# A graph layer kernel: constants projected first, x3 and x5 on another queue, and another split of the last tile

## The reference, cut to what matters

```python
h = maximum(layernorm(x), 0.0)                        # rows
xn = batchnorm(h, norm1_g, norm1_b)                   # columns
agg = segment_sum(xn[src], dst) / maximum(deg, 1)
conv_out = relu(agg @ W_conv + b_conv)
# linear attention over the first 256 rows, 8 heads of 64, 256 random features (proj)
q, k, v = h_dense @ Wq, h_dense @ Wk, h_dense @ Wv
qf, kf = phi(q, True), phi(k, False)                  # exp(u - diag - max) / 16 + 1e-6
attn = (qf (kf^T v)) / (qf sum(kf)) @ Wo
out = x + batchnorm(conv_out + attn[batch, pos] + h, norm2_g, norm2_b)
```

## Time and profile before

| | |
|---|---|
| median of 3 runs | 175.11 us (174.8 to 175.3) |
| profiled execution | 174.95 us, of which the span of instructions 173.1 us |
| busy: PE, PEld, DVE, ACT, POOL | 96%, 63%, 80%, 52%, 4% of the span |
| granted TensorE clock, mean | 0.99 |
| DMA | 13.71 MB, 79 GB/s on average, up to 350 GB/s in the head |

### The profile page before, as it was taken

One profiled execution on the slowest core, in us unless ns is written; L12 is line 12 of the kernel. 1 busy time (PEld: TensorE's weight loads), 2 busy tenths in 40 slices (PEclk: granted clock), 3 DMA queues, 4 the chain that ended last, 5 costly groups with the idle time before them and its releaser, 6 DMA issues.

```text
span 173.1 us, 3035 instructions
## 1 busy us (share of the span) xinstructions
PE 166.0 (96%) x1135; PEld 109.6 (63%) x1136; DVE 138.3 (80%) x317; ACT 89.8 (52%) x163; POOL 7.6 (4%) x22
## 2 busy tenths in 40 slices
PE   7999999999999999999999999999999999999980
PEld 2588887545545546557767797684464574777960
DVE  3987989899947786999656785976999998597980
ACT  3228998749793789969506164218600505004060
POOL 5047000000000000000000000000000000000000
PEclk9999999999999999999999999999999999999996
DMA  5999960000800000000000000000395004050046
GB/s 169 353 342 284 310 221 0 0 4 0 251 12 0 4 0 0 0 4 2 0 4 0 0 4 0 0 4 4 94 315 187 0 27 121 6 146 2 0 118 183
DMA packets 12412, 13.71 MB, mean 79 GB/s; under 512 B 1474, under 2 KB 7788, under 8 KB 12396
## 3 DMA queue, kind: packets, MB, share of 16 engines
q1 hardware_dynamic: 11116, 12.18, 22.4%
q10 hardware_dynamic: 960, 1.05, 1.8%
q0 software_dynamic: 320, 0.26, 0.7%
HBM read 10.92 MB, written 2.56 MB: 78 GB/s over the span
## 4 chain that ended last, share of the span: by engine, by line
PE 88%; DVE 6%; ACT 2%; issue 1%; DVEq 0%; ACTq 0%
PE bank L992 22%; PE bank L715 20%; PE bank L645 8%; PE bank L666 4%; PE bank L739 4%; PE bank L729 4%; PE bank L758 4%; PE bank L797 4%; PE bank L692 4%; PE bank L657 3%; PE bank L637 3%; PE bank L703 2%; PE bank L1020 2%; DVE r L1412 1%; DVE r L1407 1%
## 5 line engine op out<-in xcount | busy, mean ns | idle before, releaser
L992 PE MATMUL bank<-r,gh 128*128 128x512 f16 (+8 forms) x140 | 39.3, 314 | 0.0
L992 PE MATMUL bank<-r,gl 128*128 128x512 f16 (+8 forms) x140 | 39.3, 313 | 0.0
L715 PE MATMUL bank<-wc,xs 128*128 128x512 f32 (+1 forms) x80 | 38.5, 608 | 0.2 <-DVE gl L1243 0.2
L1100 DVE TENSOR_TENSOR ohb<-iota,bcol 128x1280 f16<-128x1280 f16 x25 | 20.5, 819 | 3.7 <-PE bank L657 3.7
L715 PEld LDWEIGHTS bank<-wc,xs 128*128 128x128 f32 (+1 forms) x80 | 13.6, 187 | 11.6 <-issue 11.6
L398 ACT ACTIVATE r<-bank 128x500 f16<-128x500 f32 x25 | 18.3, 765 | 3.4 <-PE bank L657 3.4
L992 PEld LDWEIGHTS bank<-r,gh 128*128 128x128 f16 (+1 forms) x140 | 13.5, 97 | 8.5 <-issue 0.3
L992 PEld LDWEIGHTS bank<-r,gl 128*128 128x128 f16 (+1 forms) x140 | 13.6, 97 | 8.2
L613 ACT ACTIVATE bw<-mv,epst 128x1 f32<-128x1 f32 x4 | 1.2, 295 | 31.0 <-DVE mv L1418 31.0
L645 PE MATMUL bank<-hT,r 128*128 128x256 f32 x64 | 14.6, 383 | 0.0
L657 PEld LDWEIGHTS bank<-ohv,ohb 128*128 128x128 f16 x250 | 9.7, 98 | 6.6 <-issue 5.3
(11 more groups left out here) (179 smaller groups left out, 269.1 us busy)
## 6 DMA issues: line engine op xcount, KB each, us to landing
xs<-in_x SPq DMA_DIRECT2D x15, 256.0 KB, 5.0
out<-xs SPq DMA_DIRECT2D x7, 256.0 KB
r<-in_L_gnn_Wq SPq DMA_DIRECT2D x2, 512.0 KB, 7.2
r<-in_L_gnn_Wk SPq DMA_DIRECT2D x1, 1024.0 KB, 5.6
wc<-in_L_gnn_W_conv SPq DMA_DIRECT2D x1, 1024.0 KB, 9.6
wvo<-in_L_gnn_Wv SPq DMA_DIRECT2D x1, 1024.0 KB, 12.8
wvo<-in_L_gnn_Wo SPq DMA_DIRECT2D x1, 1024.0 KB, 5.2
xs<-in_x ACTq DMA_DIRECT2D x3, 256.0 KB, 4.4
```

What stands on the lines that cost most here:

```text
L715: last = nc.tensor.matmul(acc[0:n, :], xnT[:, f, i * P:i * P + n], wc[:, f, :], start=(f == 0), stop=(f == FT - 1))
L992: last = nc.tensor.matmul(acc[:, 0:cn], gg[0:n, s, f * P:(f + 1) * P], A16[0:n, s, c0:c0 + cn], start=(s == 0 and gg is gh), stop=(s == NT ...
L1100: last = V.tensor_tensor(oh[:, s0:s0 + n, :].rearrange("p s (m t) -> p s m t", t=2), iota16[:, 0:size].rearrange("p (m t) -> p m t", t=2). ...
```

## The change

In the head: the filler is 15 long. project_consts is the first thing behind it, ahead of the first edge search, and takes the first bank. ScalarE copies its bank, behind the stores of tiles 1 and 0. ScalarE issues x1, the five vectors and proj; SP issues x3 and x5 behind the first half of Wq and no longer issues vectors and proj.

In the middle: TensorE loads the flag between heads_out(0) and heads_out(1); the branch stays behind both.

In the tail: of tile 2, parts 1 and 2 are turned plainly, then part 0 with the residual. VectorE sums (2,2) between moments and scale. Of tile 3, VectorE scales 512 to 1023, ScalarE 0 to 255, 256 to 511 and the rest, and the parts are turned in the order 0, 1, 2 with waits to match. SP stores tile 2's parts in the order 2, 0, 1. The last 98 rows of tile 3 are stored by ScalarE.

```diff
-ROUSE, ROUSE_NEXT = 18, 1
+ROUSE, ROUSE_NEXT = 15, 1
-        order = [("first",), ("hT", 1), ("hT", 0), ("q", 0), ("q", 1), ("hT", 2), ("hT", 3), ("hT", 4), ("hT", 5),
-                 ("consts",), ("k", 0), ...
+        order = [("consts",), ("first",), ("hT", 1), ("hT", 0), ("q", 0), ("q", 1), ("hT", 2), ("hT", 3), ("hT", 4), ("hT", 5),
+                 ("k", 0), ...
-        order_end += [...] + [("zT", FT - 2, j) for j in (0, 2, 1)]
+        order_end += [...] + [("zT", FT - 2, j) for j in (1, 2, 0)]
@@ SP
-            load_x(2)
-            load_x(4)
+            for i in (3, 5, 2, 4):
+                load_x(i)
...
-            for k, v in enumerate((g1, b1, g2, b2, b_conv)):
-                sp.dma_start(vrow[4 * k:4 * k + 4, :], v.rearrange("(t p) -> t p", p=P)).then_inc(vec_in, 16)
-            for k in range(2):
-                sp.dma_start(pj[:, :, k * DH:(k + 1) * DH], proj.rearrange("(t p) d -> p t d", p=P)).then_inc(pj_in, 16)
...
-                for j in {FT - 2: (0, 2, 1), FT - 1: (0, 2)}.get(f, (0, 1, 2)):
+                for j in {FT - 2: (2, 0, 1), FT - 1: (0, 2)}.get(f, (0, 1, 2)):
...
-                        for i in range(8, NT):
+                        for i in range(8, NT if f < FT - 1 else 9):
@@ ScalarE
-            for i in (1, 3, 5):
-                act.dma_start(xs[:, i, :], x[i * P:(i + 1) * P, :]).then_inc(x_in[i], 16)
+            act.dma_start(xs[:, 1, :], x[P:2 * P, :]).then_inc(x_in[1], 16)
+            for k, v in enumerate((g1, b1, g2, b2, b_conv)):
+                act.dma_start(vrow[4 * k:4 * k + 4, :], v.rearrange("(t p) -> t p", p=P)).then_inc(vec_in, 16)
+            for k in range(2):
+                act.dma_start(pj[:, :, k * DH:(k + 1) * DH], proj.rearrange("(t p) d -> p t d", p=P)).then_inc(pj_in, 16)
...
             store_hT(0)
+            acc = landed(act, "consts")
+            act.activation(pT[:, :], acc[:, 0:M], ACT.Copy)
+            act.activation(vec[:, :], acc[:, M:M + 20], ACT.Copy).then_inc(read("consts"), 1)
...
                     copy_turned(f - 1, 0)
-                    copy_turned(f - 1, 2)
                 act.wait_ge(st2_ready, f + 1)
-                for a, b in ... else ((512, 768), (768, 1024), (1024, N)):
+                for a, b in ... else ((0, 256), (256, 512), (1024, N)):
...
+            stored(act, "zT", FT - 1, 2)
+            act.dma_start(out[(NT - 1) * P:N, c], xs[0:LAST, NT - 1, c]).then_inc(o_out, 16)
@@ TensorE
             rouse(ROUSE)
+            pe.wait_ge(id_set, 1)
+            project_consts()
             edge_search(0)
-            pe.wait_ge(id_set, 1)
...
             transpose_h(5)
-            project_consts()
...
             heads_out(0)
+            pe.wait_ge(flag_ready, 1)
+            covered = pe.value_load(flag[0:1, 0:1], min_val=0, max_val=1)
             heads_out(1)
-            uncovered_edges()
+            uncovered_edges(covered)
...
-                    elif j == 0:
+                    elif j == 1:
                         pe.wait_ge(z_dve, 1)
...
-                        if f == FT - 1 and i in (4, 6):
-                            pe.wait_ge(z_act, 3 * f + i // 2 - 1)
+                        if f == FT - 1 and i in (0, 2):
+                            pe.wait_ge(z_act, 3 * f + i // 2 + 1)
...
+            transpose_z(FT - 2, (1, 2))
             turn_with_residual(FT - 2, 0)
-            turn_with_residual(FT - 2, 2)
-            transpose_z(FT - 2, (1,))
             transpose_z(FT - 1)
@@ VectorE
             def constants():
-                acc = landed(dve, "consts")
-                V.tensor_copy(pT[:, :], acc[:, 0:M])
-                V.tensor_copy(vec[:, :], acc[:, M:M + 20]).then_inc(read("consts"), 1)
                 stored(dve, "consts")
...
                 moments(f)
+                finish(f - 1, 2)
                 scale(f)
                 dve.wait_ge(st2_ready, FT)
-                V.tensor_scalar(yT[:, f, 0:512], yT[:, f, 0:512], s2[:, f:f + 1], t2[:, f:f + 1],
+                V.tensor_scalar(yT[:, f, 512:1024], yT[:, f, 512:1024], s2[:, f:f + 1], t2[:, f:f + 1],
```

More of the change, by code:

```diff
@@ L202, in gnn_kernel @@
             order_end += [("agg", f, 0), ("agg", f, 1)] + [("zT", f - 1, j) for j in range(3)] + [("agg", f, 2)]
-        order_end += [("agg", FT - 1, c) for c in range(len(LAST_CHUNKS))] + [("zT", FT - 2, j) for j in (0, 2, 1)]
+        order_end += [("agg", FT - 1, c) for c in range(len(LAST_CHUNKS))] + [("zT", FT - 2, j) for j in (1, 2, 0)]
         order_end += [("zT", FT - 1, j) for j in range(3)]
@@ L615, in _ @@
                     copy_turned(f - 1, 0)
-                    copy_turned(f - 1, 2)
                 act.wait_ge(st2_ready, f + 1)
-                for a, b in ((0, 512), (512, 1024), (1024, N)) if f < FT - 1 else ((512, 768), (768, 1024), (1024, N)):
+                for a, b in ((0, 512), (512, 1024), (1024, N)) if f < FT - 1 else ((0, 256), (256, 512), (1024, N)):
                     act.activation(yT[:, f, a:b], yT[:, f, a:b], ACT.Identity,
@@ L760, in heads_out, with uncovered_edges @@
                 last.then_inc(full("ha", i), 1)
-            def uncovered_edges():
-                pe.wait_ge(flag_ready, 1)
-                covered = pe.value_load(flag[0:1, 0:1], min_val=0, max_val=1)
+            def uncovered_edges(covered):
                 with pe.If(covered == 0):
@@ L998, in turn_with_residual @@
                 pe.wait_ge(z_act, 3 * f + j + 1)
-                for i in range(4 * j, min(4 * j + 4, NT)):
-                    n = rows_of(i)
+                for i in range(4 * j, 4 * j + 4):
                     pe.wait_ge(x_in[i], 32)
@@ L1003, in turn_with_residual @@
                     nc.tensor.matmul(acc[:, o:o + P], yT[:, f, i * P:(i + 1) * P], ident[:, :], start=True, stop=False)
-                    last = nc.tensor.matmul(acc[:, o:o + P], ident[0:n, :], xs[0:n, i, f * P:(f + 1) * P], start=False, stop=True)
+                    last = nc.tensor.matmul(acc[:, o:o + P], ident[:, :], xs[:, i, f * P:(f + 1) * P], start=False, stop=True)
                 last.then_inc(full("zT", f, j), 1)
```

## The result

The changed kernel takes 183.25 us (183.12 to 183.36, 4 runs) against 175.11 us (4 runs as well): a ratio of 1.0466, 95% interval 1.0448 to 1.0485. It is 8.1 us slower. The forecast was 175.2 with a range of 174.3 to 176.4; the time lies far outside it. Where executions of one kernel lie more than 1.5% apart, its ratio goes by the shorter ones. The profiled execution took 183.33 us, with a span of 181.4 us against 173.1.

The account below looks back on a forecast made before the run. TensorE was taken as the bound, carrying 88% of the chain of waits. From 174.95 us profiled, head 0.0, flag load -0.15 and tail +0.3 gave 175.1; with the median 0.16 higher, 175.25, stated as 175.2, range 174.3 to 176.4.

Parts of the forecast that it names:

- The landing of proj: Head: proj lands 4.4 us after issue, at 7.7 us (ends 6.8 and 9.7); net zero at the first Wk matmul.
- the late rival: Head: proj lands from 8.5 to 9.7 us and TensorE waits in project_consts, 176.0 to 177.2 us; chance 0.25.
- The round-robin rule: Head: DMA engines alternate between queues with work, so proj on a nearly empty queue could land before 7.13 us.
- the early rival: Head: proj landed by 7.13 us, transposes start at about 7.75, head gain capped near 0.55, 174.3 us; chance 0.22.
- The rest of the head: Filler, moved loads, ScalarE's issues and copies, banks: zero net; Wk caps any head gain at about 0.6 us.
- The flag load: Between the halves of heads_out: gain of 0.15 us from the 0.34 us gap, bounds -0.34 and +0.2.
- The tail: After the last sums' inputs change: reciprocal 0.2 us later, last three sums 0.5 later, net +0.3 us (+0.1 to +0.5).
- The clock rival of the tail: Tail: TensorE idles 2 us, its clock falls, ten transposes run at 1.2 GHz, +0.5 us, 175.7 us; chance 0.13.

Follow-up runs that it names:

- e7: The changed kernel without the five vector loads, their tile filled with ones: 175.03 us (profiled) and 178.94 us (not profiled).
- e4: The changed kernel with the filler 39 long in place of 15: 178.87 us, ratio 1.0197 to the kernel before.
- e5: The kernel before with only the loads moved as in the change, projection late and filler 18 as before: 176.91 us, ratio 1.0068.
- e9: e5 once more, against the kernel before: 175.55 us (10 runs), ratio 0.9992.
- e8: The kernel before with projection in the head, early flag load, proj loaded by SP ahead of Wq, vectors on ScalarE, filler 17: 174.86 us, ratio 0.9965.
- e2: The kernel before with the edits of the tail alone: 175.40 us, ratio 0.9995.
- e3: The kernel before with only the flag load moved between the two halves of heads_out: 174.55 us, ratio 0.9956.
- e1: The kernel before with the edits of the head alone, flag load and tail as before: 184.19 us, ratio 1.0507.
- e6: The changed kernel with proj issued ahead of the five vectors on ScalarE's queue: 176.51 us (profiled) and 179.63 us (not profiled).

## Why the prediction was wrong

**The landing of proj.** This is the step that failed: "I take 4.4, because proj too stands behind one load only and is small: it lands at 3.3 + 4.4 = 7.7 us". It landed 7.9 us after its issue, at 11.54, and the upper end that I allowed, 6.4 us, was too low as well. The five vectors were counted as issue time on ScalarE, 0.31 us each, and not as loads in front of proj. With them gone proj landed 3.9 us earlier (e7). "Behind one load only" was false of my own edit: six stood in front. I had a row of a proj load issued behind the same vectors: on SP's full queue it took 7.2 us, which gives 3.3 + 7.2 = 10.5 us and the late rival. It would have come near by luck, since there proj's packets began ahead of the vectors' (shown at e7).

**The round-robin rule.** The page DMA: Bandwidth & Descriptors of the Trainium skill (Queues, rings and completion order) says that an engine goes round the queues that have work, and I let it carry the early rival, at 0.22. It speaks of queues against each other. The wait arose within ScalarE's queue: 40 packets in 3.2 us, and no packet of proj among them (e7). The trace agrees with the rule as far as it goes: once proj moved, its 0.13 MB shared the engines with 1.33 MB of SP's and took nearly four us. That is no quick passage either, on a queue that held nothing else.

**The late rival.** Its mechanism was right and named: the new wait of TensorE in project_consts, with all else behind it. Its price, a us lost for a us of waiting, was half of the truth. With the wait alone the ratio was 1.0197 (e4), 178.6 us for 175.11, where the rival's own sum for a landing at 11.5 us says 179.0. (The rival's middle was also set wrong: between 176.0 and 177.2 it is 176.6, not 176.3, and the stated range ended at 176.4.) What was missing is the clock. I looked for a fall of the clock in a pause of TensorE, from the very row that shows it, but only in the tail. A pause of 5.5 us in the head with the filler shortened was the larger risk; before, the filler had run up to 7.77 us with no pause behind it. The fall cost 4.7 us (e4).

**The rest of the head.** Not shown: that three filler matmuls fewer are no loss in themselves. The filler ended at 6.15 us in this execution, not at 7.13, since the clock rose earlier than in the one before, and that made the pause longer. Right: ScalarE's first square root at 5.55, on time in spite of its eight issues, with its copies of the constants in idle time, and x3 and x5 in time for VectorE. Whether the moved loads cost anything is open (e5, e9). Right also: that Wk caps a gain of the head, at 19.2 us in e8. That the change makes x7 land later is not shown. Wk, which waits for x7, was issued at 12.48 us before and at 13.57 in the change, but at 13.44 in e2 and 13.28 in e3 too, which leave the head as it was; Wk held TensorE there as well, until 19.28 and 19.16 us.

**The flag load.** Forecast 0.15 us of gain from a gap of 0.34; measured 0.5 in the trace, and 0.4 to 1.1 us by the interval of e3. "I take -0.15, since the gap is shared by two instructions" was a guess. The gap went with the load while the branch stayed, and the gap itself is not always 0.34: three other executions had 0.56 to 0.58 (e3). A load in the middle opened no gap of its own.

**The tail.** The steps were right nearly to the tenth: reciprocal later by 0.14 (forecast 0.2), sum (3,0) 1.70 us behind scale and shift (1.7), idle time of 0.56 us before it (0.5), last sums 0.5 later. The price was not: +0.3 forecast, none that shows (e2: -0.4 to +0.25 us by its interval). The stores behind the sums took it back. The clock rival of the tail did not come about: the clock stayed at 1.00 through TensorE's pause, which was 1.27 us and not the forecast 2.

## What to carry to other kernels

Count what stands in front of a load on its own queue in loads too, not in bytes or issue time alone: here five loads of 2 KB delayed the next one by 3.9 us. When a wait moves into the head of a kernel, price what the pause does to its clock along with the pause itself, and keep filler in front of it until the data is there. And put a load into a register where matmuls are queued behind it: here it cost nothing that shows with 16 of them, and a gap of 0.33 to 0.58 us without.

## What the runs showed of the hardware

TensorE's clock after a pause is not a matter of its length alone. In the changed kernel's profile it fell 5.0 us after the filler's end. In e1's, where the filler ended at 7.51 us, it fell 3.0 us after it (the stretches behind the filler; the mean of 0.75 in the second puts the fall in its middle):

```profile
7.50:10.00 2.50, 0.01 (x1) 0.00 (x0) 2.27 (x4) 0.31 (x1) 0.00 (x0) 1.00 1.06 364
10.00:11.00 1.00, 0.00 (x0) 0.00 (x0) 0.24 (x1) 0.00 (x0) 0.00 (x0) 0.75 1.10 373
```

Pauses of 2.8 us (e6) and 1.4 us (e7) left it up in the profiled executions. At the end of the kernel before, it fell 1.6 us after the last matmul; in e5, whose tail is the same, it was still up 4.3 us after it:

```profile
168.60:172.90 4.30, 0.00 (x0) 0.00 (x0) 0.57 (x2) 0.00 (x0) 0.00 (x0) 1.00 0.72 200
```

What makes the difference stays open. Every execution of the change had a low mean clock, 0.963 to 0.966. In the profile it stayed down for ten us, though TensorE was busy for more than nine of them.

Loads on one queue do not always run in the order of their issue: in the kernel before, proj's packets began ahead of those of the vectors, which SP had issued first (shown at e7).
